# Context stage of a Perceiver block: t's first pass and the values on 64-column halves, the deviations' round trip through memory issued by ScalarE, no loops

## The reference

```
v = layernorm(x) @ Wv.T + bv              # 128 wide
t = ctx @ Wt.T + bt                       # 128 wide
dots = einsum('bih,bjh->bij', v, t)
x = x + dots / max(|v_i| * |t_j|, 1e-8)
```

## Time and profile before

| | |
|---|---|
| median of three executions | 495.64 us (494.65 to 496.19) |
| the profiled execution | 494.51 us |
| its span, first to last instruction | 492.7 us |
| granted TensorE clock, whole span | 1.000 |
| TensorE busy | 97% of the span |
| VectorE, ScalarE, GpSimd busy | 68%, 67%, 50% |
| HBM | 57.61 MB read, 11.35 MB written |

### The profile page before, as it was taken

How to read it: one execution, slowest core, us unless ns; L and a number is a source line. 1 busy time by engine, 2 the same in 40 slices (tenths; PEclk the granted TensorE clock), 3 DMA queues, 4 the chain that set the end, 5 groups by cost and what they waited for, 6 DMA issues and landing times.

```text
span 492.7 us, 13958 instructions
## 1 busy us (share of the span) xinstructions
PE 479.8 (97%) x4290; PEld 384.0 (78%) x4291; DVE 335.6 (68%) x1021; ACT 331.6 (67%) x804; POOL 243.9 (50%) x428
## 2 busy tenths in 40 slices
PE   8999999999999999999999999998999999999996
PEld 6544444567888888888888888877898999999995
DVE  3577665657788989999898999998573333333332
ACT  2765666569988998898898889886553334333432
POOL 3468764344444456474655657472555333233333
PEclk9999999999999999999999999999999999999999
DMA  8989997500001223313322221227465876675631
GB/s 305 284 195 298 297 311 207 177 2 2 1 2 39 51 88 98 98 61 87 100 57 91 67 59 51 67 84 227 152 220 160 266 229 203 207 232 192 193 131 37
DMA packets 35025, 69.32 MB, mean 141 GB/s; under 512 B 6592, under 2 KB 21826, under 8 KB 34960
## 3 DMA queue, kind: packets, MB, share of 16 engines
q1 hardware_dynamic: 31168, 59.40, 40.3%
q0 software_dynamic: 3360, 8.84, 4.8%
q10 hardware_dynamic: 432, 0.26, 0.2%
HBM read 57.61 MB, written 11.35 MB: 140 GB/s over the span
## 4 chain that ended last, share of the span: by engine, by line
PE 65%; DVE 6%; issue 4%; ACT 3%; POOL 2%; POOLq 0%; ACTq 0%; DVEq 0%
PE psum L1532 13%; PE psum L1545 12%; PE psum L1459 9%; PE psum L1436 6%; PE psum L1423 6%; PE psum L1415 6%; PE psum L1383 5%; PE psum L1488 5%; PE psum L1282 5%; DVE arena L912 1%; POOL tok L528 1%; POOL out L614 1%; ACT arena L1145 0%; DVE smax L901 0%; ACT arena L1181 0%
## 5 line engine op out<-in xcount | busy, mean ns | idle before, releaser
L1532 PEld LDWEIGHTS psum<-arena,ring 128*128 128x128 f32 x608 | 73.5, 192 | 2.6 <-issue 0.6
L1532 PE MATMUL psum<-arena,ring 128*128 128x128 f32 x608 | 74.1, 275 | 0.5 <-issue 0.5
L1545 PE MATMUL psum<-w_s,arena 128*128 x304 | 71.9, 380 | 0.0
L1215 ACT ACTIVATE arena<-psum 128x256 f32<-128x256 f32 x38 | 14.6, 385 | 81.7 <-PE psum L1282 74.8
L1036 DVE SCALAR_TENSOR_TENSOR arena<-psum,slot_rec,arena 128x256 f32<-128x256 f32 x38 | 18.4, 484 | 69.3 <-PE psum L1545 69.0
L556 POOL TENSOR_TENSOR ov<-o_n,v_s 128x256 f32<-128x256 f32 x32 | 26.1, 817 | 77.8 <-DVE o_n L794 77.8
L1545 PEld LDWEIGHTS psum<-w_s,arena 128*128 128x128 f32 x304 | 55.0, 190 | 6.1
L1181 ACT ACTIVATE arena<-kT,head_mask 128x256 f32<-128x256 f32 x128 | 59.3, 531 | 0.0
L614 POOL DMA_INDIRECT out<-arena,token_of x38 | 38.8, 1022 | 19.0 <-POOL token_of L606 14.1
L901 DVE TENSOR_REDUCE smax<-psum 128x16 f32<-128x1024 f32 x32 | 39.2, 1224 | 12.6 <-PE psum L1436 12.6
L1145 ACT ACTIVATE arena<-arena 128x1024 f32<-128x1024 f32 x32 | 33.8, 1057 | 19.0 <-DVE arena L912 18.9
(11 more groups left out here) (206 smaller groups left out, 1072.9 us busy)
## 6 DMA issues: line engine op xcount, KB each, us to landing
ring<-w SPq DMA_DIRECT2D x38, 512.0 KB
w_s<-ctxT SPq DMA_DIRECT2D x15, 768.0 KB, 8.5
w_s<-w SPq DMA_DIRECT2D x16, 448.0 KB, 3.4
slot_rec<-routed SPq DMA_DIRECT2D x38, 132.0 KB
tok<-x SPq DMA_DIRECT2D x16, 256.0 KB, 7.8
w_s<-xT SPq DMA_DIRECT2D x12, 256.0 KB, 6.8
routed<-pad_rec SPq DMA_DIRECT2D x1, 1980.0 KB, 8.6
tok<-b SPq DMA_DIRECT2D x14, 128.0 KB, 3.1
```

The lines of the kernel that those rows point to most:

```text
L1532: mm = pe.matmul(hid_bank(p)[:, f * P:(f + 1) * P], w1_s[:, r, c * F + f * P:c * F + (f + 1) * P], xgT[:, p, c * P:(c + 1) * P], start=c = ...
L1545: mm = pe.matmul(bank(2 + q, D), hidT[:, q, f * P:(f + 1) * P], w2_s[:, bass.ds(e * (FC * D) + f * D, D)], start=f == 0, stop=f == FC - 1)
```

## The change

Five edits, all in the context stage:

1. In steps 4 to 15 each of t's first-pass matmuls, and each of the values' matmuls, becomes two, one on columns 0 to 63 of the array and one on columns 64 to 127, with the same moving data.
2. The write of a pair's deviations and the read back into all partitions are issued by ScalarE instead of SP, at the end of its step: in step t the read back of pair t+2, which waits for the landing of its write, and then the write of pair t+3.
3. `std_b` has four slots (SPREAD) instead of two, with four semaphores for each direction; `wvc_s` moves behind it.
4. The four engines lay all steps out one by one (`lay_steps`) where one round of a loop stood.
5. SP's step holds only loads.

```diff
+SPREAD = 4
-        std_b = arena[:, 2048:2048 + 4 * P].rearrange("p (s j) -> p s j", s=2)
-        wvc_s = arena[:, 2048 + 4 * P:2048 + 4 * P + KC * H].rearrange("p (c h) -> p c h", c=KC)
+        std_b = arena[:, 2048:2048 + 8 * P].rearrange("p (s j) -> p s j", s=SPREAD)
+        wvc_s = arena[:, 3328:3328 + KC * H].rearrange("p (c h) -> p c h", c=KC)
...
-                if not turned(i - 2):
-                    spread_deviations(i - 2, k % 2)
...
-                if not turned(i):
-                    need(sp, s["a_std"], i - TURNED + 1)
-                    sp.dma_start(deviations[bass.ds(i, 1)].rearrange("o p h -> (o p) h"), pair_std[:, bass.ds(i * 2, 2)])\
-                        .then_inc(std_out[k % 2], 16)
...
-            run_steps(pool, context_step, -4, NB - 1, 6, 10)
+            lay_steps(context_step, -4, NB - 1)
...
-                    need(dve, std_in[p], arrivals(v - TURNED, p, 2, 16))
+                    r = (k + 1) % SPREAD
+                    need(dve, std_in[r], arrivals(v - TURNED, r, SPREAD, 16))
...
+            def write_deviations(n):
+                act.wait_ge(s["a_std"], n - TURNED + 1)
+                act.dma_start(deviations[n], pair_std[:, n * 2:(n + 1) * 2]).then_inc(std_out[n % SPREAD], 16)
+
+            def spread_deviations(n):
+                q = n % SPREAD
+                act.wait_ge(std_out[q], arrivals(n - TURNED, q, SPREAD, 16))
+                need(act, s["v_sbuf"], n - SPREAD + 1)
+                act.dma_start(std_b[:, q, :], deviations[n:n + 1].rearrange("o p h -> o (p h)").broadcast_to([P, 2 * P]))\
+                    .then_inc(std_in[q], 16)
...
                     act.activation(tsq[:, p, :], both, ACT.Square, bias=xbt_s).then_inc(s["t_sbuf"], 1)
+                if TURNED <= t + 2 < NB:
+                    spread_deviations(t + 2)
+                if TURNED <= t + 3 < NB:
+                    write_deviations(t + 3)
...
-                    pe.matmul(t_bank(p, 0), wt_s[:, 0, :], ctx_in_sb[:, k, 0:2 * SC], start=True, stop=False)
+                    halved = not (isinstance(t, int) and t < TURNED)
+                    def first_pass(b):
+                        moving = ctx_in_sb[:, k, b * 2 * SC:(b + 1) * 2 * SC]
+                        if not halved:
+                            pe.matmul(t_bank(p, b), wt_s[:, 0, :], moving, start=True, stop=False)
+                            return
+                        for h in (slice(0, RG), slice(RG, P)):
+                            pe.matmul(t_bank(p, b)[h, :], wt_s[:, 0, h], moving, start=True, stop=False)
+                    first_pass(0)
...
-                    pe.matmul(t_bank(p, 1), wt_s[:, 0, :], ctx_in_sb[:, k, 2 * SC:4 * SC], start=True, stop=False)
+                    first_pass(1)
...
-                            mm = pe.matmul(bank(p, 2 * P), wvc_s[:, c, :], xT_s[:, k, c * 2 * P:(c + 1) * 2 * P],
-                                           start=c == 0, stop=c == KC - 1)
+                            for h in (slice(0, RG), slice(RG, P)):
+                                mm = pe.matmul(bank(p, 2 * P)[h, :], wvc_s[:, c, h], xT_s[:, k, c * 2 * P:(c + 1) * 2 * P],
+                                               start=c == 0, stop=c == KC - 1)
```

More of the change, by code:

```diff
@@ L298, in build @@
         ctx_in = [sem(f"ctx_in{n}") for n in range(4)]
-        std_in = [sem(f"std_in{n}") for n in range(2)]
-        std_out = [sem(f"std_out{n}") for n in range(2)]
+        std_in = [sem(f"std_in{n}") for n in range(SPREAD)]
+        std_out = [sem(f"std_out{n}") for n in range(SPREAD)]
         rec_out = [sem(f"rec_out{n}") for n in range(RING)]
@@ L346, in load_tokens @@
                         .then_inc(ctx_in[k], 16)
-                def turned(n):
-                    return isinstance(n, int) and not TURNED <= n < NB
-                if not turned(i - 2):
-                    spread_deviations(i - 2, k % 2)
                 for n in (i + 2,) if i < 4 else (i + 2, i + 3) if i == 4 else (i + 3,):
@@ L360, in load_tokens @@
                         sp.dma_start(to, source).then_inc(s["consts_in"], 16)
[L362 to L366, removed]
             for i in range(NB):
                 load_tokens(i, i % 4)
-            for n in (NB - 2, NB - 1):
-                spread_deviations(n, n % 2)
             sp.wait_ge(s["consts_made"], CONSTS)
@@ L696, in context_step @@
                     dve.scalar_tensor_tensor(vT[:, p, :].rearrange("f (h t) -> f h t", h=2),
-                                             std_b[:, p, :].rearrange("f (t h) -> f h t", h=2), xbs_s[:, :],
+                                             std_b[:, r, :].rearrange("f (t h) -> f h t", h=2), xbs_s[:, :],
                                              bank(p, 2 * P).rearrange("f (h t) -> f h t", h=2), ALU.mult, ALU.add)\
@@ L914, in attention_step @@
                         .then_inc(s["centred"], 1)
-            run_steps(dve, context_step, -4, NB - 3, 6, 10)
+            lay_steps(context_step, -4, NB - 3)
             attention_step(-1, 3)
@@ L1202, in attention_step @@
                     spread_second_values((k - 1) % 2, (k - 1) % 4)
-            run_steps(act, context_step, -1, NB, 4, 12)
+            lay_steps(context_step, -1, NB)
             context_step(NB, NB)
@@ L1511, in attention_step @@
                     turn_output(y, (k - 3) % 2)
-            run_steps(pe, context_step, -1, NB, 8, 12)
+            lay_steps(context_step, -1, NB)
             pe.wait_ge(s["consts_made"], CONSTS)
```

## The result

The changed kernel took 514.02 us (median of 6 executions, 509.67 to 518.18), the kernel before 495.79 us on the same chip (494.26 to 497.91). The ratio is 1.035 [1.031, 1.038]: slower by 3.5%. The forecast was 494.0 us, with a range of 492.8 to 498.0: wrong, in sign too. The profiled execution took 518.18 us (span 516.4) and counts as a slow one, while the ratio is of fast executions alone. Its waits so add up to more than the median shows.

The account below looks back on a forecast made before the run. TensorE's own stream was taken to bound the context stage. Form changes saved 2.0 us in steps 4 to 13, step 14 lost 0.34, all else nothing: net 1.66 off 495.64 gives 493.98 us, range 492.8 to 498.0.

Parts of the forecast that it names:

- the one on the landing: Context stage, ScalarE's queue: a deviation write lands in some 4 us, so the spread's wait costs nothing.
- its own limit of 5.3: ScalarE's queue: up to 5.3 us of landing, the turn of spread and write fits a 5.74 us step.
- a rival with 0.12: Landing too late at the spread's wait in ScalarE's queue: at 6.35 us +7, 502.7 us; chance 0.12.
- The change of form: TensorE, context stage: each array form change costs 0.20 us; one of three per step goes, saving 2.0 in steps 4 to 13.
- the streams of the halves: TensorE, first pass and values: streaming on column halves takes as long as on the full array, no difference.
- the 1.66: Context stage: net gain in us from column halves, all steps together.
- Steps 14 and 15: TensorE: step 14 loses 0.14 + 0.20 = 0.34 us; step 15 saves 0.20 and loses 0.20.
- The issues: ScalarE's 24 added issues lie beside its evictions, costing 0; rival that they aren't hidden: 496.3 us, chance 0.11.
- Weights of the halves: TensorE: weight loads of the halves stay hidden; rival that they don't: +5.8, 499.7 us, chance 0.05.
- No loops: Context stage: laying the steps out without loops changes nothing, since each loop goes round once.
- VectorE's ring: VectorE's cycle through cos, statistics, norms: 5.71 us a turn, under the 5.74 step; rival 5.85, 494.7 us, chance 0.11.
- VectorE's waits for the spread: VectorE waits for spread deviations, 2.2 us in four places, vanish but lie off the path: worth nothing.

Follow-up runs that it names:

- run 5: Changed kernel, steps written out, the spread reading rows of x without waiting for the write to land (values wrong): 494.29 us, ratio 0.992.
- run 11: Changed kernel, steps written out, ScalarE still writing the deviations but SP reading them back in its old place: 493.99 us, ratio 0.996.
- run 7: Changed kernel, steps written out, the write issued ahead of the waiting spread, both still at the step's end: 500.28 us, ratio 1.004.
- run 1: Kernel before, steps written out, first pass and values on column halves in steps 4 to 15, SP moving the deviations: 494.85 us, ratio 0.997.
- run 12: Kernel before without its loops, only t's first pass on column halves, values on the full array, SP moving the deviations: 496.52 us, ratio 1.001.
- run 4: Kernel before, steps written out, column halves in steps 4 to 13 only, SP moving the deviations: 493.95 us, ratio 0.996.
- run 8: Kernel before with the four loops of the context stage written out, nothing else: 498.31 us, ratio 1.001.
- run 9: Changed kernel, steps written out, from step 4 on the write issued two steps ahead of its spread: 501.09 us, ratio 1.009.
- run 3: Changed kernel, steps written out, the write moved from the step's end to behind Exp: 498.68 us, ratio 1.006.
- run 6: Changed kernel, steps written out, write behind Exp from step 4 on, at the step's end in steps 1 to 3: 498.59 us, ratio 1.002.
- run 10: Changed kernel, steps written out, write two steps ahead from step 4 on, halves in steps 4 to 13 only: 500.20 us, ratio 1.009.

## Why the prediction was wrong

**The step that failed** is the one on the landing: "I take some 4 us", under its own limit of 5.3. It measured 6.9 at the median, 4.8 at the least and 10.4 at the most, so that all but one of the twelve were over the limit. The mechanism, its place and the limit were right, as a rival with 0.12. By that rival's own reckoning 6.9 gives (6.9 + 0.45 - 5.94) x 10 - 1.6 = +12.5, 508 us; 514 were measured. The turns were 7.50 us on average, 11 of them, where the rival's would be 7.35, and TensorE's clock fell behind its waits (7.0 us in the profiled execution, 3.4 of them in step 14), which no rival had.

**Where the choice went astray.** Two rows priced the landing: twelve writes of this very transfer, in this stretch, at 9.1, and one load of the same size, at 3.9, at the start. I took the second and explained the first away by the 1 MB ahead of it in SP's queue. That was argued, not shown, and runs 5 and 11 refute it: 9.0 and 7.8 us at the median with no such load ahead in the queue. Even the changed kernel's first write, at 17.83 us, with nothing ahead of it in its queue, took 7.7. The transfers from 17.5 to 23 us (queue: packets, MB, share of 16 engines):

```profile
q1 hardware_dynamic: 1092, 2.05, 100.3%
q10 hardware_dynamic: 140, 0.00, 1.4%
```

SP's loads (q1) fill the engines, and the write's packets, on ScalarE's queue (q10), start only 3.8 us after its issue and take 1.5 us. The Trainium skill (DMA: Bandwidth & Descriptors, Issuing engines are not separate DMA queues) says that transfers interleave on the same 16 engines whoever issues them, and that another issuer saves only issue time; the prediction had weighed and set this aside. The traces agree with it: 7.8 and 9.0 us from ScalarE's queue (runs 11 and 5), 9.1 from SP's; the 6.9 of the kernel after stand beside loads of 212 GB/s, not 244.

**What else was missed**: the earlier trace rows could be 9.1 us and cost nothing because SP spread a pair two steps after its write, and because the queue behind the waiting spread was SP's own. The change halved the distance and put Ln behind the wait. The prediction had both facts, but not the third, that the next write also stands behind the waiting spread and leaves late with it: run 7, which takes the write out from behind it, brings back 14 of 18 us.

**What was right.** The change of form costs 0.20 us and goes once a step (runs 1 and 12); the streams of the halves cost nothing more. Where TensorE doesn't wait (runs 5 and 11), the gain in the stage is 1.5 and 1.4 us of the 1.66. Steps 14 and 15 lose 0.2 and not 0.34 (run 4): the fold pays its 0.20 as forecast, but in the kernel before too the first pass of step 14 is dearer behind the 14-column sums (L1303 at 90.50 takes 0.94 us instead of 0.86), which the prediction left out. The issues lie beside the evictions (run 5). Weights of the halves are hidden: L1310 takes 1.72 us for four matmuls of 512 columns on halves, as much as two on the full array. The Trainium skill (TensorE: Matmul & The Clock Gate, Part 3: Packing small matmuls) has loads overlap only where the row group differs; the trace contradicts it for the new groups too. No loops: nothing (run 8). VectorE's ring is 5.71 us a turn, just under TensorE's 5.74 (run 9). VectorE's waits for the spread were put at nothing; in runs 1 and 8, where SP still spreads, TensorE stands still behind them for 0.3 and 0.8 us.

**Open.** What makes a landing long was not tried. The share of the 16 engines alone doesn't tell: it was 0.89 over the 3.9 us of the load of the earlier trace rows, and one of SP's own writes, issued at 31.31 us, landed in 3.6 us at a share of 0.88. Run 5's ratio is under run 1's (0.992 and 0.997, their intervals just apart), though it stands only 0.4 us earlier at the dots of step 15; whether SP's relief, the other chip or its wrong values give the rest was not separated.

## What to carry to other kernels

Price a round trip through memory with the landing of the same transfer in the same stretch, at its longest and not its median, and count how many steps lie between its two ends before and after the change: a wait that moves to a compute engine's queue puts all that is behind it there on the path. If it must stand there, issue the next send ahead of the wait, so that one late landing isn't handed on. Look also whether the send could leave earlier at all: here GpSimd makes the deviations only shortly ahead of their write, and an earlier place waits for them instead (runs 3 and 6). Matmuls on column halves pay only where a change of form goes without another coming (runs 1 and 12).

## What the runs showed of the hardware

- 1 KB in 128 packets of 8 bytes, 9 ns each, landed after 4.8 to 10.4 us in the kernel after, in run 11 once after 3.2 (share of the engines 0.34). The write of 17.83 had its first packet at 21.60, its last ended at 23.12 and it had landed by 25.53, when the spread went; that of 53.87: 58.67, 59.99 and 64.31. Some half of it is time ahead of the first packet, most of the rest behind the last.
- ScalarE's queue issued its transfers up to 1.2 us ahead of the start of an activation that stands before them in the program (55.26 against 56.49, run 7).
- The issue of one 1 KB write took 0.33 us at the least, 0.45 at the median of the kernel after and 0.33 at that of run 11; four took 1.43 to 2.04 us (kernel after, runs 6, 9 and 10).
- After idling for 4.2 us TensorE ran at 1.2 GHz for 4.3 us; in step 14 the granted clock was 0.56 for 7.8 us, its waits since 72 us having been 2.46 us and less.
